# A two-layer graph kernel on one core: another order of work in row 0, earlier requests for the first tiles, shifted event places, and one power in place of two

## The chip, the cores and the metric

One core of a Trainium2 chip runs the whole program. The time is the device time of one execution, in microseconds (us). The kernel before took 964.14 us (median of three runs, 962.69 to 965.74). The profiled execution took 965.12 us; its span, from the first to the last recorded instruction, is 963.3 us. PE is TensorE, DVE is VectorE, ACT is ScalarE, POOL is GpSimd, SP is SyncE, which here only issues transfers.

## What is computed

`x` is 6144 x 128, `adj` 6144 x 6144, all float32. The reference, cut to what matters:

```python
# layer 0
x_norm = layernorm(x, g_in, b_in)
gate   = hard gumbel choice from x_norm @ Wn + bn and u       # one number per row of x
view2  = (adj * gate[:, None] * gate[None, :]) @ x_norm        # first product with adj
g      = sigmoid(concat(x_norm, view2) @ Wg + bg)
fused  = g * (x_norm @ W1 + b1) + (1 - g) * (view2 @ W2 + b2)
x1     = layernorm(x + layernorm(fused + x, g_out, b_out))
# layer 1, hyperbolic
h  = proj(mobius_add(proj(mobius_matvec(weight, x1)), hyp_bias))
xt = logmap0(h)
s  = adj @ xt                                                  # second product with adj
h  = proj(expmap0(relu(logmap0(proj(expmap0(s))))))
out = layernorm(x1 + h)
```

The two products with `adj` are nearly all of the arithmetic. Everything else is a norm, a tanh, a logarithm or a small product for each row.

## The kernel before

**Tiles.** The rows of `x` form 12 chunks of 512. A tile `(c, q)` is the 512 x 512 block of `adj` for output chunk `c` and input chunk `q`, 1 MB, loaded by `load_a(n)` (L335) into one of five buffers of `A`, so the load of tile n waits until tile n - 5 is used. PE works on a tile in two halves, numbered m = 2n and 2n + 1 (`half(m)`, L1025). In row 0 of the first layer the tiles are multiplied whole, as float32 (L1019). All later tiles, but a few, are split: ACT writes a rounded high part of a half (`split_high`, L555, instruction L562), DVE the rest (`split_low`, L753, L758), and PE forms three products for each of the two blocks of the half (L1021 to L1023), six matmuls for a half.

**Row 0.** While row 0 runs, the kernel also prepares its right-hand side, chunk by chunk, in a pipeline over the engines. For chunk k: ACT asks for x (`load_x`), DVE takes statistics (`stats_pre`, L707), POOL raises them to the power -1/2 (L428), DVE forms the negative mean (L716), ACT normalizes (`normalize`, L525), PE transposes (`transposes(k)`, L1006), ACT copies out (`transposed`, L535) and stores it to DRAM (`store_xnt`), PE multiplies by the identity and Wn (`rows_and_logits(k)`, L1013), DVE begins the gate (`gate_begin`, L732), ACT takes the exponential (L540), DVE ends the gate (`gate_end`, L741 to L746), ACT scales (`gated`, L547) and rounds (`gated_high`, L553), DVE takes the remainder (`gated_low`, L750). `half(2k)` waits for `gated(k)`. The orders of each engine are written out by hand: L592 to L606 on ACT, L776 to L806 on DVE, L1065 to L1087 on PE. DVE ends row 0 with `prepare()` (L761 to L774), which readies weights and biases, and only then splits the tiles of row 1. SP sends the gates to DRAM and loads them back broadcast, with two other tiles (L388 to L395, `load_front`), for the multiplication L850 by which row 0's sum is gated.

**Loads at the start.** SP issues them in the order L371 to L385: u and four small vectors, tile 0, seven vectors broadcast to all partitions, one column, six weights, then tile 1 and the rest.

**Events.** After row 0 each engine runs one loop over m. It splits or multiplies half m and then does the events that have their place there. The places are the tables L76 to L86: `DVE_FIRST["gate"] = (3, 0)` puts the event `gate` of first-layer row c - 1 after half 24c + 3, and after 24c + 0 when c is over `LATE` = 6. The events of one row form a chain over DVE, ACT, POOL and PE: gate, l0 (PE, the small products), tanh, fuse, stats1, nm1, y1, affine, stats2, nm2, x1, tr (PE), x1t, mx (PE) for the front part; m2m, q, tq, curv0, curv1, curv2, tc, ln, k, scale, beta, xth, xtl for the hyperbolic back part, one row later. DVE and ACT run several halves ahead of PE, as far as the areas for split halves allow, so the same m is later in time on PE.

**Second layer.** `ENDS[o]` is the number of halves up to the end of the o-th output row; for the last two, o = 10 and 11, they are 472 and 486, and 486 is the number of all halves. The events of row o stand at `ENDS[o]` plus the entry of `DVE_SECOND`, `ACT_SECOND` or `PE_SECOND`: take (DVE copies the sum out), turn (PE), relu and squares (ACT, L663 to L668), floor, norms, tanh, coef, add (L971 with statistics), mean, norm, store. For o = 11 (`ON_DVE_FROM`) DVE does floor and norms itself, and POOL only takes two powers on four columns each (L470, L471).

## Time and profile before

| | |
|---|---|
| median of three runs | 964.14 us (962.69 to 965.74) |
| profiled execution | 965.12 us |
| its span | 963.3 us |
| PE busy | 912.4 us, 95% |
| DVE busy | 789.6 us, 82% |
| ACT busy | 682.2 us, 71% |
| POOL busy | 234.5 us, 24% |
| moved by DMA | 281.72 MB, mean 292 GB/s |

```profile
## 2 busy tenths in 40 slices
PE   4998998999999999999999999998999999999993
PEld 3555777777887877888888888886687878778772
DVE  4667888988898788978695875859999898989894
ACT  6775786868686666757565465666888989788972
POOL 2210211111111111111020010201100755486563
PEclk9999999999999999999999999999999999999997
DMA  7978697776868676868574674756899999999980
```

Each digit is the busy share of one fortieth of the span (24.1 us) in tenths. PEclk is the clock that TensorE was granted, in tenths of full speed. The first slices are row 0, the slices up to about 655 us are the first layer with part of the second, and the rest is the second layer alone. The last slice is the tail after the last tile. In a timeline row the bracket at the end is the time that the engine sat idle before the instruction, and what released it.

### The profile page before, as it was taken

To read this page: it belongs to the slowest core of one execution; us is meant where nothing else is said; L and a number is where in the kernel's file an instruction comes from. 1 tells how busy PE (TensorE), PEld (TensorE's weight loads), DVE (VectorE), ACT (ScalarE), POOL (GpSimd) and SP (SyncE) were. 2 spreads that over 40 slices of the span, in tenths; PEclk is the share of its full clock that TensorE was granted. 3 is DMA by queue.
4 is the path that set the end of the run, shared out by engine and by line. 5 is a ranking of instruction groups with operands and counts; after the bars stand their busy time and mean duration, and the time that the engine had idled before them with its cause. 6 is when DMAs were issued, how large, how long until landed. Compare 5 with 4: busy or idle time off the path is not lost.

```text
span 963.3 us, 12546 instructions
## 1 busy us (share of the span) xinstructions
PE 912.4 (95%) x4032; PEld 718.1 (75%) x4032; DVE 789.6 (82%) x1781; ACT 682.2 (71%) x1214; POOL 234.5 (24%) x202
## 2 busy tenths in 40 slices
PE   4998998999999999999999999998999999999993
PEld 3555777777887877888888888886687878778772
DVE  4667888988898788978695875859999898989894
ACT  6775786868686666757565465666888989788972
POOL 2210211111111111111020010201100755486563
PEclk9999999999999999999999999999999999999997
DMA  7978697776868676868574674756899999999980
GB/s 247 385 277 308 235 407 279 291 308 259 324 244 335 233 303 251 316 222 306 195 286 175 219 269 171 261 216 219 312 358 374 401 382 420 369 402 396 395 316 33
DMA packets 51825, 281.72 MB, mean 292 GB/s; under 512 B 6528, under 2 KB 8496, under 8 KB 20656
## 3 DMA queue, kind: packets, MB, share of 16 engines
q1 hardware_dynamic: 46432, 271.48, 73.9%
q10 hardware_dynamic: 5328, 9.44, 2.7%
q8 instruction: 32, 0.52, 0.2%
q14 instruction: 33, 0.27, 0.1%
HBM read 271.44 MB, written 9.46 MB: 292 GB/s over the span
## 4 chain that ended last, share of the span: by engine, by line
PE 45%; DVE 30%; DMA 8%; ACT 7%; POOL 6%; issue 4%; SPq 0%; POOLq 0%; DVEq 0%; ACTq 0%
PE PS L1021 12%; PE PS L1023 12%; PE PS L1022 12%; DVE AL L758 8%; DVE XGL L758 6%; DMA A<-in_adjT_dram 4%; DVE XTL L758 3%; PE PS L1019 2%; DVE BS L707 2%; PE PS L1110 2%; PE PS L1106 2%; POOL r_rs L452 2%; ACT AH L562 1%; POOL p_inv L452 1%; POOL SINV L476 1%
## 5 line engine op out<-in xcount | busy, mean ns | idle before, releaser
L758 DVE TENSOR_TENSOR AL<-A,AH 128x1024 fp32r<-128x1024 f32 x247 | 294.8, 1220 | 43.0 <-ACT AH L562 42.1
L562 ACT ACTIVATE AH<-A 128x1024 fp32r<-128x1024 f32 x247 | 253.0, 1058 | 106.6 <-PE PS L1023 84.4
L1021 PE MATMUL PS<-AH,XGH 128*128 128x512 f32 x344 | 137.2, 399 | 5.9 <-DVE AL L758 5.9
L758 DVE TENSOR_TENSOR XGL<-A,XGH 128x1024 fp32r<-128x1024 f32 x113 | 132.7, 1219 | 6.7 <-ACT XGH L562 6.3
L1023 PE MATMUL PS<-AH,XGL 128*128 128x512 f32 x344 | 134.1, 390 | 0.0
L1022 PE MATMUL PS<-AL,XGH 128*128 128x512 f32 x344 | 134.0, 390 | 0.0
L562 ACT ACTIVATE XGH<-A 128x1024 fp32r<-128x1024 f32 x113 | 113.1, 1056 | 14.0 <-DMA A<-in_adjT_dram 13.9
L1021 PE MATMUL PS<-AH,XTH 128*128 128x512 f32 x290 | 114.6, 395 | 2.4 <-DVE AL L758 2.3
L758 DVE TENSOR_TENSOR XTL<-A,XTH 128x1024 fp32r<-128x1024 f32 x92 | 109.8, 1221 | 5.4 <-ACT XTH L562 5.1
L1023 PE MATMUL PS<-AH,XTL 128*128 128x512 f32 x290 | 113.0, 390 | 0.0
L1022 PE MATMUL PS<-AL,XTH 128*128 128x512 f32 x290 | 112.8, 389 | 0.0
L452 POOL TENSOR_TENSOR r_rs<-r_v,NHALF 128x4 f32<-128x4 f32 x24 | 44.3, 1847 | 266.5 <-DVE r_v L713 266.5
L562 ACT ACTIVATE XTH<-A 128x1024 fp32r<-128x1024 f32 x92 | 94.3, 1056 | 12.1 <-PE PS L1023 11.2
L1021 PE MATMUL PS<-XGH,XTH 128*128 128x512 f32 x226 | 91.1, 403 | 4.3 <-DVE XGL L758 4.2
L1023 PE MATMUL PS<-XGH,XTL 128*128 128x512 f32 x226 | 88.2, 390 | 0.0
L1022 PE MATMUL PS<-XGL,XTH 128*128 128x512 f32 x226 | 88.1, 390 | 0.0
L1021 PEld LDWEIGHTS PS<-AH,XGH 128*128 128x128 f32 x344 | 64.6, 188 | 21.8 <-DVE AL L758 8.1
L1021 PE MATMUL PS<-XTH,XGH 128*128 128x512 f32 x184 | 75.3, 409 | 3.1 <-DVE XTL L758 3.0
L1023 PEld LDWEIGHTS PS<-AH,XGL 128*128 128x128 f32 x344 | 64.6, 188 | 13.7
L1022 PEld LDWEIGHTS PS<-AL,XGH 128*128 128x128 f32 x344 | 64.7, 188 | 12.6
L1023 PE MATMUL PS<-XTH,XGL 128*128 128x512 f32 x184 | 72.5, 394 | 0.0
L1022 PE MATMUL PS<-XTL,XGH 128*128 128x512 f32 x184 | 72.4, 393 | 0.0
(245 smaller groups left out, 1560.7 us busy)
## 6 DMA issues: line engine op xcount, KB each, us to landing
A<-in_adjT_dram SPq DMA_DIRECT2D x243, 1024.0 KB, 6.8
GB<-gate_scratch SPq DMA_DIRECT2D x12, 256.0 KB, 3.6
XNT<-xnt_scratch SPq DMA_DIRECT2D x12, 256.0 KB, 4.1
XR<-in_x_dram SPq DMA_DIRECT2D x12, 256.0 KB, 4.8
x_scratch<-X SPq DMA_DIRECT2D x12, 256.0 KB, 7.7
xnt_scratch<-XNT ACTq DMA_DIRECT2D x6, 256.0 KB, 7.0
xnt_scratch<-X1T ACTq DMA_DIRECT2D x6, 256.0 KB, 6.2
XR<-in_x_dram ACTq DMA_DIRECT2D x4, 256.0 KB, 8.3
```

The costliest lines, as they stand in the source:

```text
L452: g.tensor_tensor(dst, src, NHALF[:, 0:src.shape[-1]], ALU.pow).then_inc(S[done], 1)
L476: link(g.tensor_tensor(sinv, sr, NHALF[:, :], ALU.pow))
L562: a.activation(high(m), A[:, n % RING, h * HW:(h + 1) * HW], ACT.Copy).then_inc(S["hi"], 1)
L707: last = v.bn_stats(BS[:, t, :], src[:, blk(t)])
L758: v.tensor_tensor(low(m), A[:, n % RING, h * HW:(h + 1) * HW], high(m).bitcast(F32), ALU.subtract).then_inc(S["lo"], 1)
L1019: return p.matmul(acc, whole(q)[:, blk(t)], A[:, m // 2 % RING, t * CW:(t + 1) * CW], start=start, stop=stop)
L1021: p.matmul(acc, hi[:, st], high(m)[:, mv], start=start, stop=False)
L1022: p.matmul(acc, hi[:, st], low(m)[:, mv], start=False, stop=False)
L1023: return p.matmul(acc, lo[:, st], high(m)[:, mv], start=False, stop=stop)
L1106: p.matmul(E[:, t, 0:2 * P], XNT[:, blk(t)], RX[:, :], start=False, stop=False)
L1110: last = p.matmul(E[:, t, right], GB[:, blk(t)], RS[:, right], start=False, stop=True)
```

## The change

- Tables: nearly all first-layer events get another place, most of them one half later; the second-layer tables get a second entry for the last two rows (o = 10 and 11), nearer to the row's end. The power of the final norm becomes an event `rs` of its own.
- Loads: tile 1 is asked for beside tile 0, ahead of the vectors; tiles 2 to 4 ahead of the weights.
- POOL takes one power on eight columns for the last row, where it took two on four; DVE signals once.
- Row 0: on ACT the first exponential (which loads a table) comes ahead of `load_x(3)`; on DVE `stats_pre(2)` comes ahead of `gate_begin(0)`; on PE `half(2k)` comes ahead of `transposes(k + 2)`, and `half(2k + 1)` ahead of `rows_and_logits(k + 2)`.

```diff
--- before.py
+++ after.py
@@ -73,17 +73,18 @@
 LATE = 6
 RELOAD_AFTER = 4
 CLOSE = 12
-DVE_FIRST = {"m2m": (5, 0), "part": (4, 2), "gate": (3, 0), "q": (7, 0), "fuse": (9, 5), "stats1": (9, 7),
-             "nm1": (10, 9), "resid": (10, 9), "curv0": (14, 3), "affine": (11, 10), "stats2": (13, 10),
-             "curv1": (18, 13), "nm2": (14, 12), "curv2": (18, 13), "tc": (20, 15), "k": (20, 19), "beta": (22, 21),
+DVE_FIRST = {"m2m": (6, 1), "part": (7, 3), "gate": (4, 1), "q": (7, 1), "fuse": (10, 6), "stats1": (10, 8),
+             "nm1": (11, 9), "resid": (13, 9), "curv0": (14, 4), "affine": (13, 11), "stats2": (13, 11),
+             "curv1": (17, 15), "nm2": (14, 13), "curv2": (17, 15), "tc": (20, 16), "k": (20, 19), "beta": (22, 21),
              "xtl": (24, 22)}
-ACT_FIRST = {"mx": (2, 0), "tq": (9, 2), "tanh": (9, 5), "y1": (13, 10), "x1": (19, 14), "x1t": (19, 21),
-             "ln": (20, 16), "scale": (21, 21), "xth": (24, 23)}
-PE_FIRST = {"l0": (2, 0), "tr": (14, 12), "mx": (21, 19)}
-
-DVE_SECOND = {"take": 2, "floor": 8, "norms": 16, "coef": 16, "add": 19, "mean": 24}
-ACT_SECOND = {"relu": 7, "tanh": 15, "norm": 28, "store": 30}
-PE_SECOND = {"turn": 1}
+ACT_FIRST = {"mx": (3, 1), "tq": (9, 3), "tanh": (10, 6), "y1": (13, 11), "x1": (19, 15), "x1t": (19, 21),
+             "ln": (20, 17), "scale": (23, 21), "xth": (24, 23)}
+PE_FIRST = {"l0": (3, 1), "tr": (14, 13), "mx": (21, 19)}
+
+DVE_SECOND = {"take": (2, 2), "floor": (8, 5), "norms": (16, 8), "coef": (16, 10), "add": (19, 14), "mean": (24, 17),
+              "rs": (19, 14)}
+ACT_SECOND = {"relu": (7, 4), "tanh": (15, 10), "norm": (28, 20), "store": (30, 21)}
+PE_SECOND = {"turn": (1, 1)}
 
 
 def split_homes(halves, nch):
@@ -324,7 +325,7 @@
             out = {}
             for o, end in enumerate(ENDS):
                 for event, after in table.items():
-                    out.setdefault(end + after, []).append((event, o))
+                    out.setdefault(end + after[o >= NCH - 2], []).append((event, o))
             return out
 
         def last_place(*tables):
@@ -373,15 +374,18 @@
             for t, v in ((GINC, g_in), (BINC, b_in)):
                 sp.dma_start(t[:, :], v.rearrange("(p o) -> p o", o=1)).then_inc(S["norm_vecs"], 16)
             sp.dma_start(IW[:, P:P + 2], wn).then_inc(S["norm_vecs"], 16)
-            load_a(0)
+            for n in range(2):
+                load_a(n)
             for t, v in ((HB[:, :], b_hyp), (B4[:, 0:P], b1), (B4[:, P:2 * P], bg), (B4[:, 2 * P:3 * P], b2), (B4[:, 3 * P:], b1),
                          (GOUT[:, :], g_out), (BOUT[:, :], b_out)):
                 sp.dma_start(t, v.partition_broadcast(P)).then_inc(S["vecs"], 16)
             sp.dma_start(HBC[:, :], b_hyp.rearrange("(p o) -> p o", o=1)).then_inc(S["vecs"], 16)
+            for n in range(2, 5):
+                load_a(n)
             for t, v in ((RX[:, 0:P], w1), (RX[:, P:2 * P], wg[0:P, :]), (RS[:, 0:P], w2),
                          (RS[:, P:2 * P], wg[P:2 * P, :]), (RS[:, 2 * P:3 * P], w2), (WH, w_hyp)):
                 sp.dma_start(t, v).then_inc(S["weights"], 16)
-            for n in range(1, NCH + 3):
+            for n in range(5, NCH + 3):
                 load_a(n)
             for n in range(NCH + 3, NT):
                 c, k = n // NCH, n % NCH
@@ -467,8 +471,7 @@
                 e = {k: t[:, o % 2, :] for k, t in third.items()}
                 sr, sinv = SR[:, o % 2, :], SINV[:, o % 2, :]
                 if event == "floor" and o >= ON_DVE_FROM:
-                    pow_half("s2max", 1, sinv[:, BLK:], sr[:, BLK:], "s2inv")
-                    pow_half("s2max", 2, sinv[:, 0:BLK], sr[:, 0:BLK], "s2inv")
+                    pow_half("s2max", 1, sinv, sr, "s2inv")
                 if event == "floor" and o < ON_DVE_FROM:
                     pool.wait_ge(S["sq3"], o + 1)
                     pool.nop(nofuse=True)
@@ -488,7 +491,7 @@
                     link(g.tensor_scalar(e["cf"], e["th"], MAX_NORM, None, ALU.min))
                     link(g.tensor_tensor(e["cf"], e["cf"], e["rc"], ALU.mult))
                     g.tensor_tensor(e["coef"], e["cf"], e["w"], ALU.mult).then_inc(S["coef"], 1)
-                if event == "add":
+                if event == "rs":
                     pow_half("v3", o + 1, e["rs"], e["v"], "rs3")
 
             events, results = first_places(DVE_FIRST), second_places(DVE_SECOND)
@@ -575,10 +578,10 @@
             gumbel_ln(0)
             normalize(0)
             gumbel_ln(1)
+            act.wait_ge(S["const"], 1)
+            a.activation(JUNK[:, 0:1], NHALF[:, 0:1], ACT.Exp)
             load_x(3)
             transposed(0)
-            act.wait_ge(S["const"], 1)
-            a.activation(JUNK[:, 0:1], NHALF[:, 0:1], ACT.Exp)
             store_xnt(0)
             normalize(1)
             gate_exp(0)
@@ -786,9 +789,9 @@
                                    in0=U[:, :].rearrange("p (b k) -> p b k", k=2), scalar=-1.0,
                                    in1=BNB[:, :].rearrange("p (o k) -> p o k", o=1).to_broadcast([P, NB, 2]),
                                    op0=ALU.mult, op1=ALU.add).then_inc(S["gumbel"], 1)
+            stats_pre(2)
             dve.wait_ge(S["gumbel"], 1)
             gate_begin(0)
-            stats_pre(2)
             gate_end(0)
             neg_mean_pre(2)
             stats_pre(3)
@@ -945,15 +948,14 @@
                     for t in range(BLK):
                         last = v.bn_aggr(MV3[:, i, t, :], BS[:, t, :])
                     link(last)
+                    link(v.tensor_tensor(e["v"], MV3[:, i, :, 0], MV3[:, i, :, 0], ALU.mult))
                     dve.wait_ge(S["sq3"], o + 1)
-                    v.tensor_scalar(SR[:, i, BLK:], SR[:, i, BLK:], MIN_NORM2, None, ALU.max).then_inc(S["s2max"], 1)
-                    link(v.tensor_tensor(e["v"], MV3[:, i, :, 0], MV3[:, i, :, 0], ALU.mult))
+                    link(v.tensor_scalar(SR[:, i, BLK:], SR[:, i, BLK:], MIN_NORM2, None, ALU.max))
                     link(v.tensor_tensor(e["v"], e["v"], MV3[:, i, :, 1], ALU.add))
                     v.tensor_scalar(SR[:, i, 0:BLK], e["v"], float(P), MIN_NORM2, ALU.mult, ALU.max).then_inc(S["s2max"], 1)
                 if event == "norms" and o >= ON_DVE_FROM:
                     dve.wait_ge(S["s2inv"], 1)
-                    link(v.tensor_tensor(e["nr"], SINV[:, i, BLK:], SR[:, i, BLK:], ALU.mult))
-                    dve.wait_ge(S["s2inv"], 2)
+                    v.tensor_tensor(e["nr"], SINV[:, i, BLK:], SR[:, i, BLK:], ALU.mult)
                     link(v.tensor_scalar(e["w"], SINV[:, i, 0:BLK], ATANH_MAX_NORM, 1.0, ALU.mult, ALU.min))
                     link(v.tensor_tensor(e["nr"], e["nr"], e["w"], ALU.mult))
                     v.tensor_scalar(e["t"], e["nr"], MIN_NORM, None, ALU.max).then_inc(S["n3"], 1)
@@ -1067,14 +1069,14 @@
             transposes(1)
             rows_and_logits(1)
             for k in range(NCH):
+                if k + 1 < NCH:
+                    half(2 * k)
                 if k + 2 < NCH:
                     transposes(k + 2)
                 if k + 1 < NCH:
-                    half(2 * k)
+                    half(2 * k + 1)
                 if k + 2 < NCH:
                     rows_and_logits(k + 2)
-                if k + 1 < NCH:
-                    half(2 * k + 1)
             pe.wait_ge(S["gates"], NCH)
             pe.wait_ge(S["pre_xt"], NCH)
             p.transpose(PS[0:NB, 7, 0:P], GATE[:, :], ident).then_inc(S["gate_tr"], 1)
```

## Rows read from the trace of the kernel before

**Rows 1.** The page, part 1: busy time, share of the span and instructions of each engine.

```profile
PE 912.4 (95%) x4032; PEld 718.1 (75%) x4032; DVE 789.6 (82%) x1781; ACT 682.2 (71%) x1214; POOL 234.5 (24%) x202
```

**Rows 2.** Busy time by stretch: stretch and length; PE, PEld, DVE, ACT, POOL; clock, DMA, GB/s.

```profile
12.00:14.00 2.00, 1.05 (x6) 0.75 (x6) 1.27 (x7) 1.55 (x5) 0.00 (x0) 1.00 0.19 57
...
80.00:85.00 5.00, 3.87 (x11) 3.13 (x12) 4.39 (x4) 5.00 (x7) 0.00 (x0) 0.71 0.66 226
...
500.00:550.00 50.00, 50.00 (x232) 41.34 (x232) 32.51 (x64) 26.54 (x42) 3.87 (x3) 1.00 0.58 213
...
650.00:700.00 50.00, 44.50 (x199) 34.12 (x198) 45.89 (x102) 36.40 (x58) 7.18 (x4) 1.00 0.72 259
```

**Rows 3.** Timeline of PE in row 0: start, us, engine, line, what, count, [idle before].

```profile
19.42 3.62 PE L1019 MATMUL PS<-A,FULL 128*128 128x512 f32 x4
...
68.69 1.06 PE L1013 MATMUL PS<-IW,X1T 128*128 128x130 f32 x8
69.59 5.31 PE L1019 MATMUL PS<-A,FULL 128*128 128x512 f32 x12
```

**Rows 4.** Timeline of DVE in row 0, its loop with ACT (L741 begins `gate_end`).

```profile
19.97 0.16 DVE L741 TENSOR_TENSOR SM<-LG 128x4 f32<-128x4 f32 x1
...
25.68 0.16 DVE L741 TENSOR_TENSOR SM<-LG 128x4 f32<-128x4 f32 x1
...
62.57 0.16 DVE L741 TENSOR_TENSOR SM<-LG 128x4 f32<-128x4 f32 x1
...
66.98 0.69 DVE L750 TENSOR_TENSOR XGL<-FULL,XGH 128x512 fp32r<-128x512 f32 x1 [1.86 <-ACT XGH L553]
67.59 0.16 DVE L741 TENSOR_TENSOR SM<-LG 128x4 f32<-128x4 f32 x1
```

**Rows 5.** DMA issues from 8.2 to 8.5 us, and timelines of DVE and SP.

```profile
XR<-in_x_dram ACTq DMA_DIRECT2D x1, 256.0 KB, 8.8
...
17.15 0.87 DVE L707 BATCH_NORM_STATS2 BS<-XR 128x6 f32<-128x128 f32 x4 [1.11 <-DMA XR<-in_x_dram]
...
15.09 60.17 SPq L343 DMA_DIRECT2D A<-in_adjT_dram  x15
```

**Rows 6.** Timelines of DVE and PE where row 1 begins.

```profile
79.76 4.63 DVE L758 TENSOR_TENSOR XTL<-A,XTH 128x1024 fp32r<-128x1024 f32 x4
88.50 0.69 DVE L850 TENSOR_TENSOR GB<-PS,GB 128x512 f32<-128x512 f32 x1 [4.11 <-DMA XR<-in_x_dram]
...
81.13 0.47 PE L1021 MATMUL PS<-XTH,XGH 128*128 128x512 f32 x1 [2.35 <-DVE XTL L758]
...
89.45 0.32 PE L1105 MATMUL PS<-BP,ones 128*128 128x384 bf16 x1 [2.36 <-DVE GB L850]
```

**Rows 7.** Waits from 95 to 340 us: engine, line <- releaser: us in total, times, longest.

```profile
PE PS L1021 <- DVE AL L758: 5.1, 7, 2.0
...
PE PS L1105 <- DVE GB L850: 1.1, 2, 0.7
```

**Rows 8.** Timeline of DVE in row 12, waiting for a power on eight columns.

```profile
681.59 0.17 DVE L897 TENSOR_TENSOR p_t<-p_n,p_inv 128x8 f32<-128x8 f32 x1 [0.39 <-POOL p_inv L452]
```

**Rows 9.** Powers on POOL, by line: duration in ns min/median/max, first and last start.

```profile
L452 POOL TENSOR_TENSOR p_inv<-p_n,NHALF x13: 1846/2476/2477, 111.2 to 715.1; 128x8 f32<-128x8 f32 x11, 128x4 f32<-128x4 f32 x2
...
L476 POOL TENSOR_TENSOR SINV<-SR,NHALF x11: 1658/1667/8144, 746.7 to 936.4; 128x8 f32<-128x8 f32 x11
```

**Rows 10.** Timelines of DVE, ACT and POOL in the tail.

```profile
947.88 1.13 DVE L971 SCALAR_TENSOR_TENSOR FU<-TH,e_coef,FU 128x128 f32<-128x128 f32 x4
...
950.51 0.88 DVE L942 BATCH_NORM_STATS2 BS<-PS 128x6 f32<-128x128 f32 x4
...
954.71 0.17 DVE L959 TENSOR_SCALAR e_t<-e_nr 128x4 f32<-128x4 f32 x1
...
948.71 0.60 ACT L663 ACTIVATE HY<-PS 128x512 f32<-128x512 f32 x1 [5.07 <-PE PS L1131]
...
952.22 1.99 POOL L452 TENSOR_TENSOR SINV<-SR,NHALF 128x4 f32<-128x4 f32 x2 [0.45 <-DVE SR L949]
```

## The prediction

> **What bounds the kernel now.** I read the busy shares first. PE is busy 95% of the span and nothing else is over 82% [rows 1], so time can only be won where PE is idle or badly fed. The table by stretch then says where that is [rows 2]: from 500 to 550 us PE is busy 50.00 of 50 us, while from 650 to 700 us it is busy 44.50 with DVE at 45.89. So the rows in the middle (two products for each load of a tile) have nothing to give, and the rows with one product have DVE nearly as full as PE. Four places remain: the start, the change from row 0 to row 1, the one-product rows, and the tail.
>
> Row 0: PE's first half begins only at 19.42 us [rows 3]. From then on PE needs, for each chunk, two halves of at most 1.77 us (5.31 us for three), one `rows_and_logits` of 0.90 us start to start and a transpose of about half that, 4.9 us in all at most [rows 3]. But `gate_end` began at 19.97 us for chunk 1 and at 67.59 us for chunk 10 [rows 4]: 47.62 / 9 = 5.29 us a chunk, and 5.02 us from chunk 9 (62.57) to 10. The pace is set by a loop between DVE and ACT: `gated_low` waits for ACT's rounding (1.86 us of waiting at 66.98), `gate_end` comes behind it on DVE, ACT's scaling waits for that gate, and ACT's normalization and next rounding come behind the scaling. One turn takes 5.0 to 5.1 us with PE and loads out of the way, more than PE needs. PE is not what bounds most of row 0.
>
> The start of that loop hangs on x of chunk 3: ACT asked for it 8.8 us before it landed, and DVE waited 1.11 us for it, until 17.15 us [rows 5]. Meanwhile the DMA engines were at 0.19 busy, 57 GB/s, from 12 to 14 us [rows 2]: the many small vector loads ahead of it, not bytes, held it up.
>
> Row 1: the first half, at 81.13 us, had waited 2.35 us for DVE, whose first split came at 79.76 us after `prepare()`. The small products at 89.45 us had waited 2.36 us for the gate, which DVE could only form at 88.50 us after 4.11 us of waiting for a load [rows 6].
>
> **The change, part by part.**
>
> *Earlier tiles.* Tile 1 was asked for at 15.09 us [rows 5], long before its use, and no row shows PE waiting for tiles 0 to 4. The gain of having them earlier is indirect: less traffic from 20 us on, which the x loads share. The price is direct. Ahead of x(3) stand now tile 1 and, by SP's pace of about 0.47 us an issue, tile 2 and perhaps tile 3. ACT also asks for x(3) later, by the table load and the exponential now put first: about 1.5 us. Those themselves are free, since ACT was idle before its first copy-out, and chunk 1 is normalized some 1 us earlier. From below: x(3) lands at 17.15 as before, if its delay was all small vectors. From above: it shares the engines with three tiles of 1 MB at the 400 GB/s of the busy stretches, 7.5 us more, 24.7 us. I take 19 us, near the lower end, since in [rows 5] the whole delay passed with the engines nearly empty, and bytes are then cheap.
>
> The Trainium skill (DMA: Bandwidth & Descriptors, "Issuing engines are not separate DMA queues") says that transfers of SyncE and ScalarE run on the same 16 engines and interleave. By that rule x(3) would pay for whatever part of the tiles is in flight, the upper end above. The row neither bears that out nor denies it, since no tile was in flight beside x(3).
>
> *Order of PE in row 0.* `half(0)` no longer stands behind `transposes(2)`. Those took some 1.1 us at the slow pace of that time, and chunk 1, normalized earlier, is through PE some 0.7 us or more before its time, so `half(0)` starts near 17 instead of 19.42. These 2.4 us are PE time, and the loop doesn't hand them on. `transposes(2)` now stand behind the slow first half (3.62 us for what later takes at most 1.77 [rows 3]) and end about 1 us later than before. Following the loop: `gate_end` of chunk 1 came 2.8 us after x(3), and that of chunk 2 at 25.68 [rows 4]. With x(3) at L the first comes at L + 2.8. Scaling and normalizing (chunk 3's x among them), rounding and `gated_low` follow, one turn of 5.1 us, so chunk 2 comes at about L + 8, which is 27.0 for L = 19: 1.3 us late. Before, PE with its slow first half stretched that turn to 5.71 us. From chunk 2 to 10 it was (67.59 - 25.68) / 8 = 5.24 us a chunk with small waits for x; at 5.1 the same eight turns give back 1.1 us. So the last `rows_and_logits`, and with it `prepare()` and row 1's first half, come when they came: 0, between -1.4 (L at 17.5 or less) and +5.7 us (L = 24.7).
>
> *The seam.* The last `rows_and_logits` is followed by two halves instead of three before the gates are transposed: 1.7 us earlier. The chain of stores and loads behind it ends 1.7 us earlier, near 86.8, and the gate at 87.5. On PE the small products move one half back (l0 from 2 to 3), a half being six matmuls, 1.4 us. Row 1 still begins near 81.1, four halves take to 88.5, and the 2.36 us wait is gone [rows 6]. PE works instead. I count -2.3 us. PE's idle time ahead of row 1 grows by the 1.7 us that row 0's halves end earlier. The clock that was granted from 80 to 85 us was 0.71 of full [rows 2], that is partly the lower of its two levels, after the 2.35 us of idleness; a longer idle stretch costs between 0 and 2 us more of that. I take 0, as the same drop is already in the row.
>
> *Shifted events, rows 1 to 6.* PE waited 5.1 us there for DVE's splits and 1.1 us for gates [rows 7]. Gate moves from 3 to 4 and l0 from 2 to 3, so their distance is the same. ACT's `mx` event (six instructions, ahead of the split of a half) moves too, and what fills in is one split. The tc event now has three splits behind curv2 instead of two, which hides the power. Against that, q follows m2m by one half instead of two, with a power on four columns between them, 1.0 us when quick (two in 1.99 us [rows 10]), and one half less of PE work stands between l0 and tr. I count half of the gate waits, -0.6 us, between -5 (nearly all of 6.2) and +4 (each of some six rows loses 0.7).
>
> *Shifted events, rows 7 to 13.* Where PE is full and DVE at 32.51 of 50 us, nothing changes. In row 12 DVE is the full engine. There curv2 goes from 13 to 15 and tc from 15 to 16, one split (1.2 us) between them instead of two. DVE waited 0.39 us already [rows 8] for a power of 2.48 us [rows 9]. It will wait 1.2 more, and half as much in row 13. Cover for that is only what DVE is ahead. I take +0.8 us, between 0 and 2.
>
> *Tail.* Before, DVE did add and statistics of row 10 after PE's last matmul, from 947.88, and so began the last row's floor at 950.51, though ACT's relu was done at 948.71 + 0.60 = 949.31 [rows 10]. With add at +14 (m = 486, after the last split) that work is done while PE still multiplies; its cover is the 6 us in which DVE had nothing to do. The floor then starts at 949.35. Statistics (0.88), aggregation (0.38 after 0.1) and four linked steps of 0.2 end at 951.5. One power on eight columns takes 1.66 us by the median of L476 [rows 9], so to 953.3; the norms' three steps end at 954.0, where e_t was at 954.71 + 0.17 = 954.88 [rows 10]. That is -0.9 us. The merging alone is no gain: the two old powers took 1.99 us together, but the first ran beside DVE's steps. If the power takes the 2.48 us of the other line, the gain is 0.1 us. The end of the chain (add, statistics, power, norm, store) is unchanged, and so is row 10's store, which now leaves earlier.
>
> Sum: 0 - 2.3 - 0.6 + 0.8 - 0.9 = -3.0 us. The profiled execution would take 965.1 - 3.0 = 962.1 us. It was 1.0 us over the median of the runs, so the median becomes 961.1 us; I write 961.0.
>
> **Rivals.**
>
> *The early tiles hold up x(3)* (slower). The loop DVE-ACT starts late and row 0 ends late. It decides from L = 19 on, each us of L costing one us of the whole, since PE has no other work. At L = 24.7 it costs 5.7 us and the sum is +2.7, 967; at 23 it is +1.0, 965. For the whole to be slower than before it takes L over 22. For it: DVE already waited for this load [rows 5]. Against it: the engines' 57 GB/s. Chance 0.15.
>
> *The slots cost DVE more than they save* (slower or nothing). In rows 1 to 6 the shorter way from m2m to q and in rows 12 and 13 the shorter way from curv2 to tc meet an engine that is 90% full: +0.7 us in each of six rows and +2. Sum: 0 - 2.3 + 4 + 2 - 0.9 = +2.8, 967 at most; half of it gives 964. Chance 0.15.
>
> *The waits go.* x(3) lands by 17.5, the x loads after 25 us get quicker as the tiles are in, and the shift fills most of PE's 6.2 us of waits in rows 1 to 6: -1.4 - 2.3 - 4 + 0.4 - 0.9 = -8.2, about 956. For it: each such wait in [rows 7] is at most 2 us, about one half of work. Against it: DVE has no more room than before. Chance 0.2.
>
> *It does nothing to the clock of the whole.* If PE's order in row 0 is all cover and the seam's wait only moves to the row's `tr`, only the tail is left: 963. This is the upper part of my forecast.
>
> **How the numbers follow.** The forecast, -1 to -5 us, has 0.5; its own range is 959 to 963. A measurement of this kernel can tell about 0.3%, 2.9 us, from no change. Of the forecast's half, 0.28 lies beyond that and 0.22 within. The quick case is all faster (0.2). The x(3) rival is slower in 0.09 of its 0.15, the slot rival in 0.07 of its 0.15, the rest within. Faster 0.48, same 0.36, slower 0.16. The range from 955.5 to 966.5 leaves out the far end of each rival.
>
> **What the profile would show.** x(3) used by DVE at 19 us, and `half(0)` near 17. `gate_end` of chunk 10 still near 67.6 us. Row 1's first half near 81 us, with more than 2.35 us of waiting before it, and the small products with next to none. The waits of rows 1 to 6 about as before, the wait for p_inv in row 12 over 1 us. In the tail one SINV of 1.66 us, starting 4.6 us after PE's last matmul. I am wrong if x(3) lands after 21 us, if row 0's last chunk moves by over 1.5 us either way, or if the waits in rows 1 to 6 halve.

## The result and the profile after

The changed kernel takes 958.98 us (median of 8 runs, 956.79 to 959.67), the kernel before 963.92 us on the same chip (8 runs, 962.69 to 967.43). The ratio is 0.9937 with a 95% interval from 0.9924 to 0.9951: 4.9 us less. The forecast was 961.0, its range 955.5 to 966.5. The profiled execution took 959.55 us, its span is 957.8 us, 5.5 less than before. One run of all those reported below, one of e4's four, took 1157.04 us at a granted clock of 0.75 instead of 0.99; e4's median of 957.64 counts it, and is 957.44 without it.

The busy time on the page of the kernel after:

```profile
PE 911.9 (95%) x4032; PEld 720.3 (75%) x4032; DVE 788.0 (82%) x1781; ACT 680.3 (71%) x1214; POOL 232.4 (24%) x201
```

The work is the same as in [rows 1], one POOL instruction less. Only its places moved. So I followed the same event through both kernels:

| event | before | after | difference |
|---|---|---|---|
| row 1's first half | 81.13 | 83.76 | +2.63 |
| its `tr` | 112.30 | 112.65 | +0.35 |
| `mx` in the seventh row of events | 406.69 | 401.19 | -5.50 |
| last `mx` | 689.27 | 684.66 | -4.61 |
| first `turn` | 742.34 | 738.92 | -3.42 |
| last `turn` | 948.02 | 943.34 | -4.68 |
| last negative mean (e_nm) | 959.54 | 953.97 | -5.57 |

Row 0 loses, the seam gives that back, rows 1 to 6 gain nearly six, rows 7 to 13 lose two, the end gains two. The sum looks like the forecast; its terms do not. These are differences of two single executions; the section on the experiments says how far each stretch varies.

**Row 0.** Timelines of ACT, DVE, PE and SP of the kernel after, and its busy time by stretch:

```profile
23.68 0.78 ACT L538 ACTIVATE XNT<-PS,BINC,GINC 128x512 f32<-128x512 f32 x1 [5.42 <-DMA xnt_scratch<-XNT]
...
26.66 0.87 DVE L710 BATCH_NORM_STATS2 BS<-FU 128x6 f32<-128x128 f32 x4 [6.94 <-DMA FU<-in_x_dram]
...
24.52 1.16 PE L1015 MATMUL PS<-IW,XNT 128*128 128x130 f32 x8 [2.54 <-ACT XNT L538]
25.55 3.30 PE L1021 MATMUL PS<-A,FULL 128*128 128x512 f32 x4
...
9.05 4.74 SPq L344 DMA_DIRECT2D A<-in_adjT_dram  x3
```

```profile
14.00:16.00 2.00, 1.25 (x6) 1.25 (x7) 1.12 (x8) 1.74 (x5) 0.00 (x0) 1.00 0.20 56
...
22.00:24.00 2.00, 0.00 (x0) 0.00 (x0) 0.00 (x0) 0.32 (x1) 0.00 (x0) 1.00 0.99 411
...
26.00:28.00 2.00, 2.00 (x4) 0.89 (x3) 1.24 (x8) 1.53 (x4) 0.00 (x0) 0.52 1.02 392
28.00:30.00 2.00, 2.00 (x7) 1.14 (x7) 1.71 (x10) 0.51 (x2) 1.01 (x1) 0.63 1.10 396
```

x of chunk 3 came at 15.7, earlier than the 17.15 of [rows 5]. What came late was the next two transfers of ACT: the store of chunk 0, for which ACT waited until 23.68, and x of chunk 4, for which DVE waited 6.94 us. Both took 13 us, asked for at 10.69 and 13.52 us. The DMA engines weren't full all that time: they were at 0.20 from 14 to 16 us and at 0.51 from 16 to 18, and at 0.96 to 1.04 only from 18 us on. So bytes in the way don't explain all of the 13 us. From 22 to 24 us none of the engines that compute but ACT did anything. TensorE had been idle and was then granted 0.52 and 0.63 of its clock, and the half at 25.55 took 3.30 us.

From chunk 2 on the loop ran in turns of 5.09 us: `gate_end` at 29.48, 34.58, 39.68, ... 70.21, against 25.68 ... 67.59 in [rows 4]. So 3.8 us late became 2.6.

**The seam.** DVE and PE where row 1 begins, the rows that answer to [rows 6]:

```profile
88.94 0.69 DVE L853 TENSOR_TENSOR GB<-PS,GB 128x512 f32<-128x512 f32 x1 [0.78 <-DMA XR<-in_x_dram]
...
83.76 0.47 PE L1023 MATMUL PS<-XTH,XGH 128*128 128x512 f32 x1 [3.58 <-DVE XTL L761]
90.93 0.34 PE L1107 MATMUL PS<-BP,ones 128*128 128x384 bf16 x1
```

The 2.36 us of waiting for the gate are gone, and the small products stand one half later. The later place wasn't needed for that: in e3 and e6 below, with the new order of row 0 and `l0` at its old place, the small products wait for no gate either (89.72 and 87.97 us).

**Rows 1 to 6.** Busy time over four rows; first the kernel before, then after:

```profile
123.00:335.00 212.00, 205.52 (x935) 164.44 (x934) 187.38 (x413) 155.34 (x246) 35.42 (x18) 1.00 0.77 299
```

```profile
123.00:335.00 212.00, 207.70 (x954) 168.19 (x953) 191.38 (x419) 157.90 (x251) 35.42 (x18) 1.00 0.75 300
```

In the same 212 us PE starts 19 more matmuls, which is 4.4 us of work at the 0.23 us from start to start of these rows, though it is idle only 2.2 us less. A row of events takes 44.08 us from gate to gate (130.92, 174.99, 219.07, 263.15), where it took 45.4 to 47.0 (129.64, 175.50, 220.90, 267.89).

**Rows 12 and 13, and the tail.** DVE waiting for powers, and the tail's chain, kernel after, for [rows 8] and [rows 10]:

```profile
678.41 0.17 DVE L900 TENSOR_TENSOR p_t<-p_n,p_inv 128x8 f32<-128x8 f32 x1 [1.53 <-POOL p_inv L456]
714.79 0.16 DVE L900 TENSOR_TENSOR p_t<-p_n,p_inv 128x4 f32<-128x4 f32 x1 [0.90 <-POOL p_inv L456]
...
942.59 0.69 DVE L939 TENSOR_TENSOR XNT<-PS,PART 128x512 f32<-128x512 f32 x1
944.66 0.89 DVE L945 BATCH_NORM_STATS2 BS<-PS 128x6 f32<-128x128 f32 x4 [0.61 <-ACT HY L666]
946.98 1.65 POOL L456 TENSOR_TENSOR SINV<-SR,NHALF 128x8 f32<-128x8 f32 x1 [3.12 <-DVE SR L955]
949.14 0.17 DVE L961 TENSOR_SCALAR e_t<-e_nr 128x4 f32<-128x4 f32 x1
```

### The profile page after: what moved, and what is told of

The parts are those of the page before. It is cut to its first block, busy times and chain, and to the rows that moved or that the text cites. A ratio compares the mean times of both kernels' runs of the same rounds, so it can differ in the third digit from the quotient of the medians.

```text
span 957.8 us, 12537 instructions
## 1 busy us (share of the span) xinstructions
PE 911.9 (95%) x4032; PEld 720.3 (75%) x4032; DVE 788.0 (82%) x1781; ACT 680.3 (71%) x1214; POOL 232.4 (24%) x201
## 4 chain that ended last, share of the span: by engine, by line
PE 59%; DVE 24%; POOL 5%; ACT 5%; DMA 3%; issue 3%; POOLq 0%; DVEq 0%; SPq 0%; ACTq 0%
PE PS L1023 17%; PE PS L1025 17%; PE PS L1024 17%; DVE AL L761 5%; DVE XGL L761 4%; DVE XTL L761 3%; POOL r_rs L456 2%; PE PS L1112 2%; PE PS L1108 2%; DVE BS L710 2%; PE PS L1021 1%; DMA FU<-in_x_dram 1%; DMA A<-in_adjT_dram 1%; ACT FULL L550 1%; PE PS L1122 1%
## 5 line engine op out<-in xcount | busy, mean ns | idle before, releaser
L1023 PE MATMUL PS<-XTH,XGH 128*128 128x512 f32 x184 | 72.4, 394 | 4.4 <-DVE XTL L761 4.4
```

The source lines that it names most:

```text
L1023: p.matmul(acc, hi[:, st], high(m)[:, mv], start=start, stop=False)
```

## The experiments

In the tables of places the first number is for rows 1 to 6, the second for the rows from 7 on. Two distances are read in each kernel: when row 1's first half starts (H below), and from there to the seventh `mx` (D; 325.56 before, 317.43 after). Medians and ratios are against runs of the kernel before on the same chip.

D holds the start of row 1, where the granted clock varies (last section). Cut at the same events in all fourteen traces (before, after, e1 to e12), the later stretches are far steadier than the whole:

| stretch | places or powers as before | as in the change |
|---|---|---|
| row 1's `tr` to seventh `mx` | 294.39 to 294.46 (before, e3, e11) | 288.36 to 288.96 (eight kernels) |
| seventh `mx` to first `turn` | 335.65 to 335.69 (eleven kernels) | 337.70 to 337.73 (after, e1, e2) |
| first to last `turn` | 205.68 (before alone) | 203.28 to 205.35 (thirteen kernels) |
| last `turn` to e_nm | 11.52 (before) | 10.62 to 10.63, and 10.36 with two powers (e11, e12) |

e6, e7 and e8, with single places put back, stand between in the first row: 289.70, 291.57 and 291.52.

### First set: which part carries the gain

**e1, old load order.**

```diff
-            for n in range(2):
-                load_a(n)
+            load_a(0)
...
-            for n in range(2, 5):
-                load_a(n)
...
-            for n in range(5, NCH + 3):
+            for n in range(1, NCH + 3):
```

> The changed kernel with the loads asked for in the old order (one tile ahead of the vectors, the rest behind the weights). Theory: the tiles 1 to 4 asked for ahead of the weights held up ScalarE's transfers (the store of chunk 0 kept ScalarE waiting 5.42 us until 23.68, x of chunk 4 kept VectorE waiting 6.94 us until 26.66), and this is the 2.6 us by which row 1 starts later: row 1's first half comes near 81 us again or before it, and the time falls by 2 to 4 us against the changed kernel, to 955 to 957. Rival: the new order of TensorE in row 0 costs the 2.6 us: then row 1 starts at 83 to 84 us here too, and the time stays within 1 us of the changed kernel.

Measured: 958.75 us, ratio 0.9937 [0.9921, 0.9954]; H 82.98, D 317.83. The stall of 6.94 us is gone, and the time is the same. DVE waits instead at other places (kernel e1, timeline of DVE):

```profile
18.02 0.87 DVE L707 BATCH_NORM_STATS2 BS<-XR 128x6 f32<-128x128 f32 x4 [3.06 <-DMA XR<-in_x_dram]
...
40.26 0.88 DVE L707 BATCH_NORM_STATS2 BS<-FU 128x6 f32<-128x128 f32 x4 [2.22 <-DMA FU<-in_x_dram]
```

The expectation fell: in this trace the tiles were not a cost on top, they moved the waits. x(3) is in use at 18.02 here and at 15.73 with the early tiles.

**e2, old order of PE in row 0.**

```diff
             for k in range(NCH):
-                if k + 1 < NCH:
-                    half(2 * k)
                 if k + 2 < NCH:
                     transposes(k + 2)
                 if k + 1 < NCH:
-                    half(2 * k + 1)
+                    half(2 * k)
                 if k + 2 < NCH:
                     rows_and_logits(k + 2)
+                if k + 1 < NCH:
+                    half(2 * k + 1)
```

> The changed kernel with TensorE's old order in row 0. Theory (row 0 is paced by the loop of VectorE and ScalarE and by the held-up transfers): row 1's first half stays within 0.5 us of 83.76, the gate of row 0 comes at the same time or up to 1.7 us later as the gates are transposed one half later; the time within 1.5 us of the changed kernel. Rival (the order costs the 2.6 us): row 1 starts near 81 us, and the time falls by 2 us or more.

Measured: 959.3 us, 0.9948 [0.9929, 0.9967]; H 84.10, D 317.8. The wait ahead of row 1 is 2.34 again and that for the gate 1.80 again, with the small products at 91.62 instead of 90.93. From 80 to 90 us, first in the kernel after, then in e2 (the third number from the end is the clock):

```profile
80.00:90.00 10.00, 6.42 (x21) 5.03 (x21) 9.07 (x12) 8.36 (x9) 0.00 (x0) 0.83 0.86 303
```

```profile
80.00:90.00 10.00, 7.49 (x28) 4.88 (x27) 8.36 (x10) 9.72 (x11) 0.00 (x0) 1.00 0.86 315
```

So row 1's first half to its `tr` takes 29.24 us in e2 and 28.89 after: the 1.80 us of waiting are back, and most of it is made up by the clock of this execution. By the trace the order is worth 0.7 us up to `tr` (113.34 against 112.65), which the two intervals can't tell apart.

**e3, old places in the first layer,** in the tables of DVE, ACT and PE.

```diff
-DVE_FIRST = {"m2m": (6, 1), "part": (7, 3), "gate": (4, 1), ...
+DVE_FIRST = {"m2m": (5, 0), "part": (4, 2), "gate": (3, 0), ...
```

> The changed kernel with all first-layer places (both columns of the three tables) as before; second-layer places, loads, row 0 order and the single power stay new. Theory: the places of rows 1 to 6 gained 5.9 us and those of rows 12 and 13 lost 2 us, and one half of the gain at the seam is theirs too: the time rises by 4 to 6 us against the changed kernel, to 963 to 965, and the distance from row 1's first half to the last transpose of row 6 is that of the kernel before. Rival: rows 1 to 6 gained because of what row 0 left behind (the state of the loads and of the splits' lead), then the time rises by less than 2 us.

Measured: 963.23 us, 0.9981 [0.9972, 0.999]; H 82.84, D 324.20. From 123 to 335 us PE starts 935 matmuls, as before. The places give 4.3 us: they carry the gain. Counted from row 1's `tr`, where the clock is full (1.00 in the rows above), it is 294.46 against 288.54.

**e4, old places from row 7 on.** The first numbers stay as in the changed kernel.

```diff
-DVE_FIRST = {"m2m": (6, 1), ... "curv1": (17, 15), ... "tc": (20, 16), ...
+DVE_FIRST = {"m2m": (6, 0), ... "curv1": (17, 13), ... "tc": (20, 15), ...
```

> The changed kernel with the second column of the first-layer tables (rows over 6) as before. Theory: the shorter way from curv2 to tc costs VectorE in rows 12 and 13, where it is full; with the old places the 2 us lost between 650 and 740 us come back: time lower by 1 to 2.5 us, 956.5 to 958. Rival: the loss there is a given of that stretch (whatever arrives earlier waits there for loads or for VectorE): no change within 0.7 us.

Measured: 957.64 us, 0.9922 [0.9906, 0.9939]; H 83.28, D 317.72, first `turn` 736.69, against 738.92. From the seventh `mx` to there it is 335.69 us against 337.73, so the late column costs 2.0 us, and the three kernels that have it show it alike. The wait for p_inv is back at 0.39.

### Second set: what in rows 1 to 6, and can the stall of row 0 be cured

All of these are e4 with one thing changed.

**e5, tiles by need.** Tiles 2 to 11 each wait until as many chunks are normalized, the weights stand behind tile 4.

```diff
-            for n in range(2, 5):
-                load_a(n)
...
-            for n in range(5, NCH + 3):
-                load_a(n)
+            for n in range(2, NCH + 3):
+                if n < NCH:
+                    sp.wait_ge(S["pre_y"], n)
+                load_a(n)
+                if n == 4:
...
```

> As e4, with the loads of row 0 spread: tiles 0 and 1 first, then the vectors, then each tile n from 2 to 11 only when chunk n - 1 is normalized, and the weights behind tile 4. Nothing else differs. Theory: ScalarE's transfers (x of chunks 3 to 5, the stores of chunks 0 and 1) are slow whenever several 1 MB tiles are in flight beside them, early in the changed kernel, later in the kernel before; with one tile a turn they land in 7 us or less, the gates of chunk 1 to 10 end at turns of 5.1 us without a gap (the first at 18.5, the tenth near 64 to 65 us), row 1's first half comes near 78 us instead of 83.3, and the time falls by 4 to 6 us against e4, to 952 to 954. Rival: the small vector loads themselves hold up ScalarE's transfers, or the loop of VectorE and ScalarE has no more to give: then row 1 starts at 82 us or later and the time stays within 1.5 us of e4.

Measured: 958.28 us, 0.9941 [0.992, 0.9962]; H 85.61. Kernel e5, DVE and the stretches around:

```profile
26.25 0.87 DVE L707 BATCH_NORM_STATS2 BS<-FU 128x6 f32<-128x128 f32 x4 [6.07 <-DMA FU<-in_x_dram]
...
30.00:35.00 5.00, 4.87 (x11) 2.44 (x10) 3.31 (x21) 3.60 (x12) 1.82 (x3) 0.50 0.54 143
```

The theory fell. x of chunk 4 is as late as before (26.25), and PE, which then waited 2.71 us for ACT's copy-out until 29.23, runs at half clock from 30 to 35 us. It never waited for a tile.

**e6, the gate's group back:** `m2m` 5, `gate` 3, ACT's `mx` 2, `l0` 2.

```diff
-"m2m": (6, 0), "gate": (4, 0), "mx": (3, 0), "l0": (3, 0)
+"m2m": (5, 0), "gate": (3, 0), "mx": (2, 0), "l0": (2, 0)
```

> As e4, with only m2m, gate, ScalarE's mx and l0 of rows 1 to 6 at their old places (5, 3, 2, 2). Theory A (the gate group carries the gain of rows 1 to 6): from row 1's first half to TensorE's mx of the sixth row the kernel before took 325.6 us (81.13 to 406.69), e4 317.7 (83.28 to 401.0); this one takes 321 or more. Theory B (ScalarE's waits for beta, the event scale, carry it): it stays within 1 us of 317.7 but for the 1.4 us wait ahead of the first small products.

Measured: 956.98 us (one run); H 82.17, D 317.73 against 317.72. By D this group gives nothing, and theory A fell. Cut at row 1's `tr` it is less plain: 0.9 us are gained ahead of it, 0.7 of them a wait at `tr` that is gone, and 0.9 lost behind it (289.70 against 288.80), so the new places of this group are worth up to 0.9 us in the later rows. One wait between ACT and DVE that the kernel before had is back here at its old size, so it costs no more than this (ACT for XTL, 1.9 us in four, from 123 to 335 us).

**e7, ACT's `scale` back:**

```diff
-"scale": (23, 21)
+"scale": (21, 21)
```

> As e4, with only the event scale of rows 1 to 6 at its old place (21 instead of 23), so that ScalarE waits for beta ahead of two splits again (0.62 us a row in the kernel before). Theory A: 317.7 us plus at most 1. Theory B: 320 or more from row 1's first half to the sixth mx.

Measured: 960.11 us (one run); H 83.28, D 320.38, 2.7 us longer. Waits from 123 to 335 us (engine, line <- releaser: us in total, times, longest), kernel before, then e7; the kernel after has none of these:

```profile
ACT HY L649 <- DVE r_beta L915: 2.5, 4, 0.6
ACT HY L615 <- DVE XTL L925: 1.9, 4, 0.7
ACT XTH L654 <- DVE HY L920: 1.8, 4, 0.5
```

```profile
ACT HY L648 <- DVE r_beta L914: 2.5, 4, 0.6
ACT XTH L653 <- DVE HY L919: 1.8, 4, 0.4
```

ACT reached `scale` before DVE had its factor, waited 0.62 us in each row, and DVE then waited for ACT's splits (8.9 us in these four rows, 5.5 in e4). Counted from row 1's `tr` it is 2.8 us too.

**e8, `resid` and `affine` back:**

```diff
-"resid": (13, 9), "affine": (13, 10)
+"resid": (10, 9), "affine": (11, 10)
```

> As e4, with resid and affine of rows 1 to 6 at their old places (10 and 11 instead of 13 and 13). Both other theories say: within 1 us of 317.7 from row 1's first half to the sixth mx. A third (VectorE's additions stood ahead of splits that TensorE waited for) says 319.5 or more.

Measured: 961.29 us (one run); H 83.03, D 321.24, 3.5 us longer. Counted from row 1's `tr` it is 2.7. But the wait that appears is one that the kernel before had only once, probably because its `nm1`, whose result ACT needs first, also stood one half earlier (0.9 us in all from 123 to 335 us; e8, the same stretch):

```profile
DVE FU L878 <- ACT FU L627: 8.6, 5, 1.7
```

So e8 shows that `affine` has to stand behind ACT's `y1`, and what it costs if not. It doesn't measure what the kernel before lost there.

### Third set: row 0 again, and the tail

**e9, e4 with all of row 0 old:** the edits of e1 and e2, and

```diff
-            act.wait_ge(S["const"], 1)
-            a.activation(JUNK[:, 0:1], NHALF[:, 0:1], ACT.Exp)
             load_x(3)
             transposed(0)
+            act.wait_ge(S["const"], 1)
+            a.activation(JUNK[:, 0:1], NHALF[:, 0:1], ACT.Exp)
...
-            stats_pre(2)
             dve.wait_ge(S["gumbel"], 1)
             gate_begin(0)
+            stats_pre(2)
```

> This kernel keeps the change's places of rows 1 to 6, its second-layer tables and its one power for the last two results, has the old places from row 7 on, and has all of row 0 as before: tile 0 alone ahead of the vectors, the rest behind the weights, the old TensorE order, the first-tile statistics of chunk 2 between the two parts of chunk 0's gate, and the exp table loaded behind chunk 0's transposition. Theory of the parts (each part of the change is worth what it was worth alone): row 1's first half comes at 81.1 us as in the kernel before, against 83.28 in the changed kernel with the same late places, all events from there on keep their distance to it but for the one wait of the first gate (1.5 us, which the TensorE order had removed), and the time is 955.0 to 956.8, below 957.64. Rival: row 1 takes up what row 0 gives, since its own end is set by vector work that waits for something else than row 0; then the seventh row's mean comes at 317.5 us and the time is 957 to 958.5.

Measured: 956.03 us (953.49 to 959.15), 0.991 [0.989, 0.9931]; H 82.31, D 317.84 (the rival's 317.5 was meant as this distance; the seventh `mx` itself came at 400.15, in e4 at 401.00). The time is in the first theory's interval, but H is not 81.1, and the interval overlaps that of e4. The same row 0 in e11 gave 82.20. So 81.13 in the profile of before was an early execution: the old row 0 ends at 81.13, 82.31 and 82.20 (mean 81.9), the new one in seven kernels (after, e3, e4, e6, e7, e8, e12) at 82.17 to 83.76 (mean 83.0). The means are 1.1 us apart, in single executions that scatter by 1.6.

**e10, all five tiles first,** then the vectors, then the weights:

```diff
-            for n in range(2):
+            for n in range(5):
                 load_a(n)
...
-            for n in range(2, 5):
-                load_a(n)
...
```

> Five tiles (5 MB) are asked for at once, then the eight vectors, then the six weights, then tiles 5 to 7; otherwise this is the kernel with the change's row 0 and early places and the old places from row 7 on. Theory 1 (what row 0 loses in the changed kernel is the meeting of tiles 2 to 4 with ScalarE's store of chunk 0 and its x of chunk 4 between 18 and 30 us; tiles that are in sooner leave the engines free for them): the store of chunk 0, asked for at 10.7, takes under 8 us instead of 12.9, x(4) lands before 22, no wait of VectorE in the middle of row 0 over 1 us, row 1's first half at 78 to 81, 953 to 955.5. Theory 2 (whatever ScalarE asks for beside several tiles takes as long as the tiles take, wherever they stand): x(3) now lands at 19 to 22 in place of 15.7, the store is as late as before, row 1's first half at 83 to 87, 957.5 to 961.

Measured: 955.52 us (952.41 to 956.46), 0.9897 [0.9879, 0.9915]; H 80.92. Kernel e10, DVE, then stretches:

```profile
15.59 0.87 DVE L704 BATCH_NORM_STATS2 BS<-XR 128x6 f32<-128x128 f32 x4 [0.64 <-DMA XR<-in_x_dram]
21.90 0.87 DVE L704 BATCH_NORM_STATS2 BS<-FU 128x6 f32<-128x128 f32 x4 [2.33 <-DMA FU<-in_x_dram]
...
14.00:16.00 2.00, 1.29 (x6) 1.29 (x7) 1.23 (x9) 1.74 (x6) 0.00 (x0) 1.00 1.01 417
...
24.00:26.00 2.00, 2.00 (x9) 1.17 (x8) 1.71 (x9) 1.02 (x3) 0.61 (x1) 1.00 0.51 120
```

Theory 1 in the main: x of chunk 4 is in use at 21.90 and H at 80.92, but the wait for it is 2.33 us, not under 1, the store of chunk 0 took 8.0 us, and the time lies at the edge of the expected 953 to 955.5. The engines are full from 14 us on instead of at 56 GB/s, and have air at 24 us, when the others are in the middle of their tiles. The interval ends below that of the changed kernel, but that kernel also has the late column. Against e4, which differs in the order of the loads alone, it is 0.9897 against 0.9922 with overlapping intervals: some 2 us better, which the runs don't settle. It is 8.5 us better than before.

Not all of the earlier start arrives. H is 2.36 us before e4's, the seventh `mx` 1.76 and the last `turn` 0.54. Part of it is the granted clock (stretch 80 to 90 us, e4, then e10):

```profile
80.00:90.00 10.00, 6.72 (x22) 5.40 (x23) 9.54 (x12) 7.76 (x9) 0.00 (x0) 0.83 0.92 298
```

```profile
80.00:90.00 10.00, 9.08 (x30) 7.18 (x31) 10.00 (x10) 6.57 (x7) 0.00 (x0) 0.67 0.93 342
```

PE had idled 3.59 us ahead of its first half in both. In e10 twelve matmuls of row 1's start stand 0.43 us apart instead of 0.23, in e4 seven, and from the first half to `tr` e10 takes 29.96 us, e4 28.92. e3 and e12 show the same with other starts (last section), so this looks like a chance of the execution rather than the early start's price; it isn't shown. The other 1.2 us are lost between the first and the last `turn`, where kernels with the same code differ by 2 us.

**e11, the second layer's places alone.** The kernel before, with the second-layer tables of the change and the event `rs`; two powers, as before.

```diff
-DVE_SECOND = {"take": 2, "floor": 8, "norms": 16, ...
+DVE_SECOND = {"take": (2, 2), "floor": (8, 5), "norms": (16, 8), ..., "rs": (19, 14)}
```

> The kernel before with the second-layer tables of the change, in which the last two results have places of their own and rs is an event of its own; both powers of the last two results stay two instructions, and row 0 and the first layer are as before. The forecast's tail term was 0.9 us, from a floor that starts earlier; that the powers are one adds little. If the places carry it, the first turn stays at 742.3 to 742.6 and the last result's chain from its take to the last norm is 0.7 to 1.0 us shorter than before: 963.0 against 963.9. Rival: the gain is in the one power (two powers of 1.0 us in a row and their two handovers), and this kernel's tail is as before within 0.2 us. A third share, the 0.97 us that TensorE waited for the last tile at 932.65, is expected to stay, since the first layer isn't changed.

Measured: 963.42 us against 963.98, 0.9998 [0.9983, 1.0013]: not to be told from no change. The trace tells more. From the last `turn` to e_nm: 947.25 to 957.61, 10.36 us; before 948.02 to 959.54, 11.52; after 10.63. The places give 1.16 us in the tail.

**e12, e4 with two powers:**

```diff
-                    pow_half("s2max", 1, sinv, sr, "s2inv")
+                    pow_half("s2max", 1, sinv[:, BLK:], sr[:, BLK:], "s2inv")
+                    pow_half("s2max", 2, sinv[:, 0:BLK], sr[:, 0:BLK], "s2inv")
```

> The changed kernel with the old places from row 7 on, and with GpSimd's power for each of the last two results as two instructions of 128x4 again, each with its own semaphore, in place of one of 128x8. Own places theory: from the take of the last result to the last norm the time is within 0.2 us of the 11.4 us that the changed kernel shows, and the whole within 0.3 us of 957.64. One-power theory: two powers of 1.0 us and their handovers in place of one of 1.66 make the tail 0.6 to 0.9 us longer.

Measured: 956.71 us (one run). From the last `turn` to e_nm 940.76 to 951.12, 10.36 us, where e4 took 10.63 (940.78 to 951.41). Kernel e12, POOL and DVE:

```profile
943.80 1.99 POOL L452 TENSOR_TENSOR SINV<-SR,NHALF 128x4 f32<-128x4 f32 x2 [2.53 <-DVE SR L949]
...
945.89 0.17 DVE L957 TENSOR_SCALAR e_w<-SINV 128x4 f32<-128x4 f32 x1 [0.88 <-POOL SINV L452]
```

Two powers are 0.27 us faster than one, and the eleven traces with one power show 10.62 to 10.63 us, the two with the new places and two powers both 10.36. The first starts 0.15 us before DVE begins to form the second's input. One power of 1.65 us starts only behind all inputs (in e4 944.43 to 946.07, with e_w at 946.18), two of 1.0 start at 943.80 (e_w at 945.89). Both theories missed: merging is a small loss.

## Why the prediction was right or wrong

| term | forecast | measured |
|---|---|---|
| row 0 | 0 (-1.4 to +5.7) | +2.6 in this execution, +1.1 over all |
| seam | -2.3 | -2.3 |
| places, rows 1 to 6 | -0.6 (-5 to +4) | -5.9 |
| places, rows 7 to 13 | +0.8 (0 to 2) | +2.1 |
| second layer up to its last `turn` | none | -1.3 |
| tail | -0.9 | -0.9 |
| sum | -3.0 | -5.6 |

The measured column is the difference of two profiled executions; it sums to -5.6, and the spans say -5.5. The medians say -4.9.

That the total came out some 2 us from the forecast is luck in part. Rows 1 to 6 were off by 5.3 us, and row 0 and rows 7 to 13 made up 3.9 of that in the other direction. Of the prediction's own three signs of being wrong one came true: row 0's last chunk moved by 2.6 us, from 67.59 to 70.21. The other two didn't: x(3) didn't land after 21 us, and the two rows of waits of [rows 7] went from 6.2 to 4.0 us, which isn't half. The last is the most instructive, since that stretch gained nearly 6 us all the same.

**Row 0: the step "with x(3) at L" failed, though what was measured lies in its range.** I priced the tiles by what they do to x(3) alone. It came early, since the vectors that held it up before now stood partly behind tile 1 (15.73 in the changed kernel, 15.59 in e10 with all of them behind five tiles, 18.02 in e1 with all of them ahead). My upper bound for x(3) was wrong in kind: it added 7.5 us of tiles to 17.15, though the engines had stood nearly empty before 17.15 and the tiles fill that time. In e10, with five tiles ahead and the engines at 1.01, x(3) was still in use at 15.59. I never asked for the next two transfers of the same engine, the store of chunk 0 and x of chunk 4, and ACT and DVE waited 5.42 and 6.94 us for these. The loop DVE-ACT did behave as worked out: turns of 5.09 us, and in every kernel row 1's first half stands 10.03 us behind the last `gate_end` (73.74 and 83.76; 72.28 and 82.31; 70.89 and 80.92). So what delays the last turns of the loop delays row 1 by as much, as the rival said, with another transfer in the part of L. The rule from the Trainium skill (DMA: Bandwidth & Descriptors, "Issuing engines are not separate DMA queues"), that the engines' transfers interleave, agrees with e10: x(3) landed 7.3 us after ACT asked for it, while the last two of the five tiles that SP had asked for earlier took 15.9 us by the median. In the kernel before, tile 0 was in flight too until 10.7 us, beside the first 2.3 us of x(3), which I had overlooked. The rule gives no price, and the 13 us of the next two transfers, partly with the engines at 0.20, don't follow from it.

A part of the +2.63 was never the change's: the old row 0 ends 1.1 us later in two other executions than in the one I had.

**The seam: right in size, and half right in cause.** The wait for the gate went, and e2 brings it back (1.80, and 2.34 ahead of row 1). The idle time ahead of row 1 grew from 2.35 to 3.58, by 1.2 us and not by 1.7. Of the two causes I named, the order of PE is enough: e3 and e6 have `l0` at its old place and no wait for the gate. Yet e2 is as fast within the error. Its first halves of row 1 ran at the full clock (1.00 from 80 to 90 us, against 0.83), which gives back most of the wait. The extra price of the clock, 0 in my sum, was 0 between the two profiled executions (0.83 in both), but over all traces the clock costs between nothing in e2 and twelve matmuls at its lower level, 2.4 us, in e10. Whether PE's order has a part in that isn't shown: the kernel before and e11, with the old order too, show 0.83.

**Rows 1 to 6: the mis-sized term, -0.6 for -5.9.** The step was "PE waited 5.1 us there for DVE's splits and 1.1 us for gates", of which I counted half of the second. Two things were wrong with it. First, I read [rows 7] as all that there was to win. Those are the waits that the matmul records show; the same view has rows of the weight loads, and they are longer (kernel before, 95 to 340 us, then the kernel after):

```profile
PEld PS L1021 <- DVE AL L758: 8.1, 7, 2.4
PE PS L1021 <- DVE AL L758: 5.1, 7, 2.0
...
PEld PS L1021 <- DVE XTL L758: 2.7, 6, 1.1
...
PEld PS L1105 <- DVE GB L850: 2.0, 2, 1.1
```

```profile
PEld PS L1023 <- DVE AL L761: 4.3, 4, 1.7
PE PS L1023 <- DVE AL L761: 4.0, 4, 1.3
...
PEld PS L1023 <- DVE XTL L761: 0.8, 1, 0.8
```

The three weight-load rows fall from 12.8 to 5.1 us, with none left for GB, while one for ACT's X rises from 1.9 to 3.0; the matmul rows from 6.2 to 4.0.

Second, I argued from how full DVE is, and not from what DVE and ACT wait for from each other. The three rows under e7, 6.2 us in four rows together, are such waits, and they stand at fixed places, so a table can remove them. Their sum isn't their worth, though: the first and third cost 2.7 us in e7, the second at most 0.9 in e6, and another wait of ACT for DVE, before its `y1` (L628, then L631), grew from 7.0 to 12.9 us with the change while the stretch gained. e3 shows that the places carry the gain: 5.7 us from row 1's `tr` to the seventh `mx` (294.46 against 288.80 in e4). e7 shows that `scale` behind `beta` is worth 2.8 of these; e6 that the gate's group, which I had made the term of, is worth 0.9 at most. The other 2 us are not settled: e8 makes a wait of its own. My rival of the slots that cost was wrong in sign here, though the wait that it named did appear (DVE for the power behind `m2m`, 2.7 us from 123 to 335 us). "The waits go" had the size here, not the cause, since [rows 7] kept most of its waits, and it was wrong in row 0.

**Rows 7 to 13: right in cause, too small.** The wait for p_inv grew from 0.39 to 1.53, as worked out, and 0.90 in row 13. With a third new wait that I had not looked for, 0.90 us for r_rs at 662.80, that is 2.9 us more of waiting, of which 2.1 reached PE; e4, without the late column, has these 2.0 us back at the first `turn`. Half as much for row 13, and a cover by DVE's lead, were hopes: DVE had no lead where PE waits for it.

**The tail: right in size, half right in cause.** The places give 1.16, the merged power takes 0.27 back. I had both in the sum as one, and said of merging only that it was no gain. The 1.3 us between the first and the last `turn` I had not seen, and they can't be put down to the change: the stretch took 205.68 us before, and 203.28 to 205.35 in thirteen kernels with the same new tables. Before, PE waited 0.97 us at 932.65 for the last tile. The wait is also in e3 (0.72, with the new tables of the second layer) and not in e11 (the same tables, old first layer); what brings it is open.

## What to carry to other kernels

When two engines hand work to each other at fixed places, read the waits between those two first, one row for each place, and move the consumer behind the producer. Then put each place back alone, since the length of a wait doesn't say what it costs. PE's own wait rows, matmuls alone, showed a fall of 2.2 us where nearly 6 were won. When loads are moved ahead, price every transfer that any other engine asks for until they are in, not only the next one; in these traces large tiles all at once and first (e10) disturbed the small ones less than the same tiles dealt out among them. And look at an untouched stretch in two or three executions before calling 1 us of it an effect: here the stretches from row 1's `tr` to the first `turn` repeat within 0.6 us, the start of row 1 within 1.6 and the second layer within 2.1.

## What the hardware did that I had not expected

- Transfers of 256 KB asked for by ACT took 12 to 14 us (the kernel after and e4) beside tiles that were dealt out among small loads, in e5 even with the engines at 0.34 (14 to 16 us) to 0.45 (16 to 18 us) after x of chunk 4 was asked for, and 7.4 to 9.0 us beside five tiles asked for at once with the engines full. Issues from 9 to 30 us, kernel after, then e10 (count, KB each, median us to landing):

```profile
FU<-in_x_dram ACTq DMA_DIRECT2D x1, 256.0 KB, 13.1
xnt_scratch<-X1T ACTq DMA_DIRECT2D x1, 256.0 KB, 13.2
```

```profile
FU<-in_x_dram ACTq DMA_DIRECT2D x2, 256.0 KB, 9.0
xnt_scratch<-X1T ACTq DMA_DIRECT2D x2, 256.0 KB, 8.8
```

  Why tiles dealt out are the worse neighbours was not settled.
- SP's three tile issues at 9.05 us held it for 4.74 us. They were no longer 0.47 us each, as I had reckoned, and in the kernel before single issues of 64 KB had already taken up to 2.54 us (at 9.22). It isn't the size of the tiles that holds SP: in e10 the issue of a column of 0.5 KB at 11.03 held it for 8.19 us, and so the weights and tiles behind it left late, which goes with the air at 24 us. What holds it is open.
- A power of POOL on eight columns took 1.65 us in the tail and one on four columns 1.0: two small ones take 0.3 us more in all, and the first can start earlier.
- The granted clock from 80 to 90 us varied between kernels that run nearly the same code there: after 3.6 us of idleness it was 0.83 in the changed kernel, e1, e4, e6, e7 and e8 (row 1 at 82.17 to 83.76), 0.67 in e10 (80.92) and 0.66 in e3 and e12 (82.84, 82.33). After 2.34 to 2.35 us it was 1.00 in e2 (84.10) and 0.83 in the kernel before, e9 and e11 (81.13, 82.31, 82.20). Neither the start of row 1 nor the idle time orders these, so it is an uncertainty of some 1 us in any single trace.
